# The low-rank layer of a four-part sequence kernel: its factors made by rank over 128 partitions, and the front's sums read out of PSUM

## The reference, cut to what matters

```python
# part 0, per batch row b (2 rows)
ae = layernorm(cond, ln_g, ln_b)                        # (2, 512)
h = gelu(ae @ w1 + b1)                                  # (2, 512)
xw = h @ w2 + b2                                        # (2, 8192), w2 is (512, 8192), 16.8 MB
x_a, x_b = split(xw, 2); each reshaped to (b, 512, 8)   # column index is d * 8 + rank
layer = base + einsum('bdr,bkr->bdk', x_a, x_b)         # (b, 512, 512)
x = x + (x + x @ layer)                                 # so 2 x + x @ layer
# part 1
x = x + tanh(x @ W_ih.T + (cond @ W_hh.T + b_hh + b_ih))
# parts 2 and 3, each: gates of x @ Wx + b + h @ Wh, 2048 steps, x = x + h of the step
```

## Time and profile before

| | us |
|---|---|
| median of 3 runs | 12192.23 |
| runs, lowest to highest | 12192.1 to 12194.81 |
| profiled execution, its own time | 12186.99 |
| profiled execution, span from first to last instruction | 12183.9 |

### The profile page before, as it was taken

One profiled execution on the slowest core, in us unless ns is written; L12 is line 12 of the kernel. 1 busy time (PEld: TensorE's weight loads), 2 busy tenths in 40 slices (PEclk: granted clock), 3 DMA queues, 4 the chain that ended last, 5 costly groups with the idle time before them and its releaser, 6 DMA issues.

```text
span 12183.9 us, 681007 instructions
## 1 busy us (share of the span) xinstructions
PE 11997.7 (98%) x429656; PEld 4439.7 (36%) x167512; DVE 7525.4 (62%) x34072; ACT 3039.0 (25%) x20584; POOL 1414.8 (12%) x5242
## 2 busy tenths in 40 slices
PE   7899999999999999999999999999999999999998
PEld 5433333333333343333343333343333343333333
DVE  4366666666666666666666666666666666666664
ACT  1122222222222222222222222222222222222221
POOL 4011111111111111111111111111111111111110
PEclk8999999999999999999999999999999999999999
DMA  4100000000000000000000000000000000000000
GB/s 147 37 6 6 6 6 6 6 6 6 6 6 6 6 6 6 6 6 6 6 6 6 6 6 6 6 6 6 6 6 6 6 6 6 6 6 6 6 6 4
DMA packets 382314, 123.89 MB, mean 10 GB/s; under 512 B 355654, under 2 KB 363910, under 8 KB 379308
## 3 DMA queue, kind: packets, MB, share of 16 engines
q1 hardware_dynamic: 364332, 46.45, 2.4%
q10 hardware_dynamic: 12544, 25.17, 0.6%
q0 software_dynamic: 2432, 8.39, 0.2%
HBM read 63.08 MB, written 16.84 MB: 7 GB/s over the span
## 4 chain that ended last, share of the span: by engine, by line
PE 96%; DVE 1%; ACT 0%; issue 0%; DVEq 0%; POOL 0%
PE gates L80 88%; PE proj L780 7%; DVE gates_t L912 0%; DVE pre L917 0%; ACT tanh_c L828 0%; ACT sig L823 0%; DVE prod L924 0%; DVE state L931 0%; DVE state L935 0%; DVE gc L927 0%; DVE state L938 0%; ACT gc L824 0%; DVEq L923 0%; DVEq L911 0%; DVE y_rows L888 0%
## 5 line engine op out<-in xcount | busy, mean ns | idle before, releaser
L80 PE MATMUL gates<-wh,state 128*12 128x256 bf16 x393216 | 11463.6, 273 | 93.4 <-DVE state L938 89.6
L80 PEld LDWEIGHTS gates<-wh,state 128*12 128x12 bf16 x131072 | 3302.1, 88 | 6625.9 <-issue 6410.2
L912 DVE STREAM_TRANSPOSE gates_t<-gates 128x256 f32<-128x256 f32 x4096 | 1843.8, 450 | 1586.1 <-PE gates L80 1581.5
L823 ACT ACTIVATE sig<-pre 128x16 f32<-128x16 f32 x4096 | 885.9, 216 | 7081.6 <-DVE pre L917 7081.6
L917 DVE TENSOR_REDUCE pre<-gates_t 128x24 f32<-128x96 f32 x4096 | 1340.4, 327 | 140.8
L924 DVE TENSOR_TENSOR prod<-sig,gc 128x16 f32<-128x16 f32 x4096 | 718.5, 175 | 1129.9 <-ACT gc L824 1028.4
L931 DVE TENSOR_TENSOR state<-sig,tanh_c 128x8 f32<-128x8 f32 x4096 | 690.5, 169 | 1123.9 <-ACT tanh_c L828 1123.9
L828 ACT ACTIVATE tanh_c<-gc 128x8 f32<-128x8 f32 x4096 | 854.3, 209 | 1711.6 <-DVE gc L927 1711.6
L840 POOL TENSOR_TENSOR x<-x1r,state 128x8 f32<-128x8 f32 x2048 | 433.3, 212 | 5436.6 <-DVE state L938 5436.6
L840 POOL TENSOR_TENSOR y<-x,state 128x8 f32<-128x8 f32 x2048 | 432.6, 211 | 5063.7 <-DVE state L938 5063.7
L819 ACT COPY gates_t<-area 128x32 f32<-128x32 f32 x4096 | 826.1, 202 | 20.5 <-POOL area L849 18.3
(11 more groups left out here) (81 smaller groups left out, 1243.5 us busy)
## 6 DMA issues: line engine op xcount, KB each, us to landing
w<-in_w ACTq DMA_DIRECT2D x8, 2048.0 KB, 16.6
out<-y_rows SPq DMA_DIRECT2D x1024, 8.0 KB, 1.9
wx<-in_x SPq DMA_DIRECT2D x16, 512.0 KB, 4.5
x_t_all<-x_t ACTq DMA_DIRECT2D x8, 1024.0 KB, 4.8
x1p<-x_t_all SPq DMA_DIRECT2D x128, 64.0 KB, 2.6
x1r<-x_t_all SPq DMA_DIRECT2D x128, 64.0 KB, 2.6
wx<-in_Wh POOLq DMA_DIRECT2D x8, 512.0 KB, 4.7
wx<-in_Wh POOLq DMA_DIRECT2D x16, 256.0 KB, 6.4
```

What stands on the lines that cost most here:

```text
L80: return pe.add_instruction(mybir.InstMatmult(name=nc.get_next_instruction_name(), engine=mybir.EngineType.PE, ins=[pe.lower_ap(moving), p ...
L823: act.activation(sig[l][:, 0:2 * HB], pre[l][:, 0:2 * HB], ACT.Sigmoid)
L912: dve.transpose(gates_t[l][:, :, NS * NB:], gates[l][:, 0:NMS * C].rearrange("p (m c) -> p m c", c=C)).then_inc(s["trans"], 1)
```

## The change

In `condition`:

- The product by `w2` puts the rank on the partitions. For rank r = 4 i + j, column tile j holds it at partition 32 j + 2 i + b for batch row b. The moving operand is `w2` read at a step of eight floats (`by_rank`); the two halves i are added into the same bank with two versions of the weights, `hid_p[:, 0]` and `hid_p[:, 1]`, whose columns are shifted by two. `b2` enters by a fifth matmul with a one-hot column (`select`). A product so has 2 x 5 x 4 = 40 matmuls of 128 columns.
- The pieces of x_b come first (`ORDER`), then those of x_a. A piece of x_b is copied out of PSUM into `xb`; a piece of x_a is copied twice, multiplied by a mask that keeps one batch row. After each piece of x_a its two layer matmuls follow over 128 partitions, and VectorE adds `base`. `xw_dram`, the stores, and the reload are gone.
- The hidden vector and the term of cond are computed with the vector as the weights and the matrix moving (`rows_by_tile`), turned once by a transpose.
- `w2` is asked for by SP, after `w1`, LayerNorm's vectors, `b1` and `b2`; x's first tile after the fourth piece, its second tile after the last. W_hh, W_ih, `b_ih`, `b_hh`, the gate biases and `base` are asked for by POOL, W_hh once `w1` and `b1` have landed.
- ScalarE loads its square root and gelu tables ahead by an activation on a spare value (`ahead`), and copies the turned W_hh and W_ih out of PSUM, which VectorE did. VectorE starts on cond's own semaphore.

In `front`: `x0_t` is made by one instruction, 2 x + PSUM; the tanh is written over its own PSUM bank, and `x1_t` is summed from there. The transposes of the next tile wait for `s_x1` in place of `s_tanh`.

The diff, cut to its core:

```diff
-    WC = W2N // NJ
-    ND = WC // RANK
+    NI = RANK // NJ
+    ND = W2N // RANK
+    HALF = NPIECE // 2
+    ORDER = [*range(HALF, NPIECE), *range(HALF)]
...
+        def by_rank(ap, i, j):
+            return ap.rearrange("p (d r) -> p r d", r=RANK)[:, NJ * i + j, :]
+        def of_piece(n):
+            return slice(ND * (n % HALF), ND * (n % HALF) + ND)
...
+                def second(k):
+                    dve.wait_ge(s_xw, k + 1)
+                    done(dve.tensor_copy(xb[:, of_piece(ORDER[k])], factor[k % 2][:, 0:ND]), f"xb{k}")
+                second(0)
+                second(1)
+                dve.wait_ge(s_term_r, 1)
+                done(dve.tensor_copy(rows[1][:, :], by_row[:, P:2 * P]), "term_r")
+                second(2)
+                dve.wait_ge(s_term_t, 1)
+                dve.wait_ge(s_bias, NBIAS * DMA)
                 for h in range(NH):
...
-                for n in range(NPIECE):
-                    dve.wait_ge(s_pe, J_XW + n)
-                    done(dve.tensor_tensor(xw[:, n, :, :], bank[4 + n % 2][:, 0:WC].rearrange("p (d r) -> p r d", r=RANK),
-                                           b2[:, n, :].rearrange("p (d r) -> p r d", r=RANK), ALU.add), f"xw{n}")
-                dve.wait_ge(s_base, DMA)
-                for k in range(NB * NH):
-                    b, h = divmod(k, NH)
-                    dve.wait_ge(s_pe, J_LAYER + k)
-                    done(dve.tensor_tensor(layer[b][:, h, :], bank[k % 4][:, :], base[:, h, :], ALU.add), f"layer{k}")
+                second(3)
+                dve.wait_ge(s_dve, V["mask"])
+                for k in range(HALF, NPIECE):
+                    n = ORDER[k]
+                    dve.wait_ge(s_xw, k + 1)
+                    for b in range(NB):
+                        step = dve.tensor_scalar(xa[:, b, of_piece(n)], factor[k % 2][:, 0:ND], mask[:, b:b + 1],
+                                                 None, ALU.mult)
+                        step.then_inc(s_factor, 1)
+                    if k == HALF:
+                        dve.wait_ge(s_base, DMA)
+                    for b in range(NB):
+                        dve.wait_ge(s_layer, NB * n + b + 1)
+                        dve.tensor_tensor(layer[b][:, n, :], bank[(NB * n + b) % 4][:, :], base[:, n, :],
+                                          ALU.add).then_inc(s_made, 1)
...
+                sp.wait_ge(s_zero, ZERO)
+                sp.dma_start(b2[0:NPIECE, :], ins["b2"].rearrange("(n i) -> n i", i=W2N)).then_inc(s_b2, DMA)
+                for k, n in enumerate(ORDER):
+                    if k >= NW2:
+                        sp.wait_ge(s_xw, k - NW2 + 1)
+                    load_blocked(sp, w2[k % NW2][:, :, :], ins["w2"][:, W2N * n:W2N * n + W2N], s_w2[k % NW2])
+                    if k == NW2 - 1:
+                        turn.load_rows(sp, 0)
                 sp.wait_ge(turn.s_turn, NH)
                 turn.load_rows(sp, 1)
...
+                pool.wait_ge(s_w1, 2 * DMA)
+                pool.dma_start(whh[:, :, :], ins["W_hh"].rearrange("(a p) i -> p a i", p=P)).then_inc(s_whh, DMA)
+                pool.dma_start(wih[:, :, :], ins["W_ih"].rearrange("(a p) i -> p a i", p=P)).then_inc(s_wih, DMA)
+                pool.wait_ge(s_zero, ZERO)
+                pool.wait_ge(s_ident, 2)
+                for i in range(NI):
+                    for b in range(NB):
+                        pool.tensor_copy(select[:, :, i, NB * i + b], ident[:, 0:NPIECE]).then_inc(s_select, 1)
+                load_bias(pool, bih_t[:, :], ins["b_ih"], s_bias)
+                load_bias(pool, bhh_t[:, :], ins["b_hh"], s_bias)
+                load_gate_bias(pool, keep["bias"][0][:, :], ins["b_l2"], s_bias)
+                load_gate_bias(pool, keep["bias"][1][:, :], ins["b_l3"], s_bias)
+                load_blocked(pool, base[:, :, :], ins["base"], s_base)
...
-                for n in range(NPIECE):
-                    if n == 1:
-                        act.wait_ge(s_w1, 2 * DMA)
-                    if n == NW2:
-                        act.wait_ge(s_dve, V["variance"])
-                        act.activation(stat[:, 3:4], stat[:, 2:3], ACT.Sqrt).then_inc(s_act, 1)
-                        act.wait_ge(s_pool, 4)
-                        act.wait_ge(s_w1, 2 * DMA)
-                        act.wait_ge(s_pe, J_HID)
-                        for h in range(NH):
-                            act.activation(hid_t[:, h, 0:NB], small[:, 32 + NB * h:32 + NB * h + NB], ACT.Gelu,
-                                           bias=b1_t[:, h:h + 1]).then_inc(s_act, 1)
-                    if n >= NW2:
-                        act.wait_ge(s_pe, J_XW + n - NW2)
-                    load_blocked(act, w2[n % NW2][:, :, :], ins["w2"][:, W2N * n:W2N * n + W2N], s_w2[n % NW2])
...
+                for k in range(4):
+                    act.wait_ge(s_turn, k + 1)
+                    act.copy(whh_t[:, k, :], bank[k][:, :]).then_inc(s_whh_t, 1)
+                for k in range(4):
+                    act.wait_ge(s_turn, 4 + k + 1)
+                    act.copy(wih_t[:, k, :], bank[k][:, :]).then_inc(s_wih_t, 1)
...
+                def rows_by_tile(out, columns, moving):
+                    for h in range(NH):
+                        for j in range(NJ):
+                            mm = pe.matmul(out[C * j:C * j + C, :], columns[:, h, :], block_cols(moving[:, h, :], j),
+                                           start=(h == 0), stop=(h == NH - 1),
+                                           tile_position=(0, C * j), skip_group_check=True)
+                    return mm
...
+                def product(k):
+                    n = ORDER[k]
+                    pe.wait_ge(s_w2[k % NW2], (k // NW2 + 1) * DMA)
+                    if 2 <= k < HALF + 2:
+                        pe.wait_ge(s_dve, V[f"xb{k - 2}"])
+                    elif k >= HALF + 2:
+                        pe.wait_ge(s_factor, NB * (ORDER[k - 2] + 1))
+                    to = factor[k % 2][:, 0:ND]
+                    for i in range(NI):
+                        for h in range(1 + NH):
+                            for j in range(NJ):
+                                columns = hid_p[:, i, h - 1, :] if h else select[:, n, i, :]
+                                moving = by_rank(w2[k % NW2][:, h - 1, :] if h else b2[:, :], i, j)
+                                mm = pe.matmul(to[C * j:C * j + C, :], columns, moving,
+                                               start=(i == 0 and h == 0), stop=(i == NI - 1 and h == NH),
+                                               tile_position=(0, C * j), skip_group_check=True)
+                    mm.then_inc(s_xw, 1)
...
+                pe.wait_ge(s_whh, DMA)
+                for k in range(4):
+                    turned(whh, k)
+                pe.wait_ge(s_b2, DMA)
+                pe.wait_ge(s_select, NI * NB)
+                pe.wait_ge(s_dve, V["hid_p"])
+                product(0)
+                pe.wait_ge(s_wih, DMA)
+                for k in range(4):
+                    pe.wait_ge(s_whh_t, k + 1)
+                    turned(wih, k)
+                product(1)
+                rows_by_tile(by_row[:, P:2 * P], cond_p, whh_t).then_inc(s_term_r, 1)
+                product(2)
+                pe.wait_ge(s_dve, V["term_r"])
+                pe.transpose(small[:, 2 * P:3 * P], rows[1][:, :], ident[:, :]).then_inc(s_term_t, 1)
+                pe.wait_ge(s_wih_t, 4)
+                turn.transpose(pe, 0, bank)
+                product(3)
+                pe.wait_ge(s_dve, V["xb3"])
                 pe.wait_ge(turn.s_copy, NH)
-                pe.wait_ge(s_back, 2 * DMA)
-                for k in range(NB * NH):
-                    b, h = divmod(k, NH)
-                    if k >= 4:
-                        pe.wait_ge(s_dve, V[f"layer{k - 4}"])
-                    pe.matmul(bank[k % 4][:, :], block_cols(xab[:, b, 0:D], h), xab[:, b, D:2 * D],
-                              start=True, stop=True).then_inc(s_pe, 1)
+                for k in range(HALF, NPIECE):
+                    n = ORDER[k]
+                    product(k)
+                    for b in range(NB):
+                        pe.wait_ge(s_factor, NB * n + b + 1)
+                        if NB * n + b >= 4:
+                            pe.wait_ge(s_made, NB * n + b - 3)
+                        pe.matmul(bank[(NB * n + b) % 4][:, :], xa[:, b, of_piece(n)], xb[:, :],
+                                  start=True, stop=True).then_inc(s_layer, 1)
...
-                                       (lambda h: pe.wait_ge(s_tanh, NH * (u - 1) + h + 1)) if u else None)
+                                       (lambda h: pe.wait_ge(s_x1, NH * (u - 1) + h + 1)) if u else None)
...
-                            step = act.activation(tanh_t[:, h, cols], banks(u, 2)[h][:, cols], ACT.Tanh,
+                            step = act.activation(banks(u, 2)[h][:, cols], banks(u, 2)[h][:, cols], ACT.Tanh,
...
```

(48 more changed lines are left out.)

133 lines of the change are left out of this document (52 added, 81 removed).

## The result

| | us |
|---|---|
| before, median of 5 runs | 12192.23 (12184.79 to 12194.81) |
| changed, median of 5 runs | 12135.34 (12133.75 to 12137.98) |
| ratio, 95% interval | 0.9954 (0.994 to 0.9969) |
| changed, profiled execution, own time and span | 12137.98, 12136.2 |

The change takes 56.9 us off the median. The forecast was 12129, the range 12115 to 12152.

A forecast was written before the change was run, and what follows sets the result against it. The recurrence, bound by TensorE, stays unedited; waits in condition and front were to shrink. Condition 30.5 us plus front 32 makes 62.5, taken as 63: 12192.2 - 63 = 12129 us, range 12115 to 12152.

The forecast's parts named there:

- Step 1: Front: sums reading one operand from PSUM take 0.69 us, so TensorE's stalls go; 32 us saved, bounds 28 to 34.
- warm start: Front's first matmuls run at full clock instead of slowly; front saving 34 us, half a microsecond added to the forecast sum.
- Step 2: Condition: with loads reordered and DMA queues kept full, the last piece of `w2` lands at 62.5 us instead of 72.9.
- Steps 3 and 4: Condition's tail after the last `w2` landing, including the price of strided reads: 7.5 us, between 5.6 and 13.
- the sign named for it: Start of the front's matmuls in the changed profile, expected at 64 to 76 us.
- Step 3: Condition after the last landing: product, masked copy, layer matmuls, base sum; 5.6 us at full clock, 9.7 at half.
- rival C: Condition: strided reads make TensorE the bound; slower than before from 12 us a product, 12231 at 17; chance 0.03 in full.
- formula 22 + 13 + 8P: End of condition if TensorE bounds it: start at 22 us, 13 for transposes and layers, eight products of P each.
- Step 5: Condition: biases and `base` asked for by POOL instead of SP stay hidden, costing nothing; bias landing between 20 and 45 us.
- Rivals A and D: Condition: POOL's bias and base loads late, 12135 to 12149; or `w2` pieces asked for late, 12144; together chance 0.16.
- B: Front: VectorE's stalls beside POOL stay, leaving 31 us of saving, 12162 us; chance 0.05.

The follow-up runs named there:

- e7: Changed kernel with the front's sum as two instructions again, each with one operand in PSUM; 12141.19 us, a single run.
- e2: New `condition` of the change with the `front` of the kernel before; 12169.98 us, ratio 0.9983.
- e8: Changed kernel with the tanh written to SBUF again, so only `x1_t`'s sum has two SBUF operands; 12136.13 us, a single run.
- e3: Changed kernel with products reading 128 adjacent columns of `w2` and `b2` instead of every eighth (wrong columns, same work); 12126.49 us, ratio 0.9947.
- e5: The changed kernel once more, unedited, on another round of runs; 12138.18 us, ratio 0.9955.
- e6: Changed kernel with TensorE's list reordered: product 0 before W_hh's transposes, products ahead of the previous piece's layer matmuls; 12132.49 us, ratio 0.9951.

## Why the prediction came out as it did

*Step 1, the front: right, a little over its upper end.* 32 us were forecast with 34 for a warm start; 34.8 came. The reason given, the pair of SBUF operands beside POOL, is shown by e7 (two instructions without the pair: no stall), e2 (the pair: 12.20 us for one) and the sums at 692 ns once POOL has stopped. Both new forms were priced at 0.69 and take 0.69. What the step had too coarse: it took the slow first tile as likely to stay, and it named the tanh as part of the remedy, which e8 shows to be worth nothing.

*Step 2, the last landing: right.* 62.5 was forecast, and the last piece landed at 62.0. The average rate from 4 to 63 us was 384 GB/s where 385 was taken. W_hh's transposes began at 18.27 (18 forecast), product 0 ended at 26.7 (27).

*Steps 3 and 4, the tail: the term that was mis-sized.* 7.5 us were forecast from the last landing to the front, between 5.6 and 13; 19.2 came, outside the step's own bounds, so condition ended at 81.2 in place of 70, and the sign named for it, front matmuls from 64 to 76 us, was missed. The forecast put a product between 2.4 and 8.0 us and took it a third of the way, at about 4.3, where 4.9 was measured; the price itself was nearly met. What failed is what was made of it: the forecast let TensorE wait for the last landing, and TensorE came to the last piece 10.8 us after it. Step 3 weighed products and layers against the 5.2 us between landings only to settle the clock, and only at 2.4 us a product. At 4.9, with 1.98 for the layers and the hand-over to the masked copy, a piece takes 7.24 us of TensorE. Four of them from 51.02 end at 80, however early `w2` is there. This is rival C's mechanism, TensorE as the bound, at a price at which the change still gains; the forecast gave C a chance only at prices that end within the noise of no change or slower. Its formula 22 + 13 + 8P with P = 4.9 gives 74.2, and what it left out are TensorE's waits: 2.57 us for x, 0.34 for `w2`, about 0.5 at each of four masked copies, 0.4 for `xb`, 1.05 to the block's end, 6.3 in all, which makes 80.5. e3 shows the size of the step without the stride: products take 2.4 us, the front begins 7.1 us after the last landing, at 69.33, and 64.0 us are gained where 63 were forecast. But even there TensorE did not wait for the last piece; its list and the landing were within about a microsecond of each other, so that the 7.5 us fit owes something to luck. VectorE's factor of 1.76 came near TensorE's 2; no run shows that the two have one cause, and the 1.76 also holds what a VectorE instruction costs at any length (a copy of 8 columns takes 0.17 us). The choice of a third was not argued from a row, and the end to which the skill's rule pointed should have been carried through the period of a piece.

*Step 5, the moved queues: right.* The six gate biases took POOL 4.75 us to ask for, not 23.32, hterm followed at 39.75 with no wait, and `base` was there for the first sum at 57.66. Rivals A and D did not happen, nor did B. A's own sum was off: 55 to 65 us and four times 4.2 and 1 make 73 to 83, not 76 to 88.

*Together*: condition gave 11.2 us less than forecast and the front 2.3 more (34.8 against 32.5 with the warm start), 8.9 us short by the profiled stages and 6.3 by the medians, inside the range, whose upper part was there for A and for the stride. That the total stands inside although condition ended 5 us outside its bounds is in part luck: the range reached to 12152 for rival A, which was not the case. The prediction also named a recurrence longer by over 5 us as a contradiction, and by the two profiles it is 6.4 longer; the same kernel again (e5) has 11810.7 and e6, with the same recurrence, 11804.3, so a difference of this size comes without an edit.

## What to carry to other kernels

When a wait for a transfer is shortened, work out the period of the loop behind it on each engine with the operands as they will be read: here a step of 32 bytes doubled TensorE's fp32 products and made TensorE the bound of the stage's second half, and the stage gave 19 us in place of the 30 forecast. Beside a busy POOL, look at where VectorE's operands lie before counting its instructions, and mend first the sum that another engine waits for. Work that stands in line behind a late transfer is worth moving ahead of it once its engine is the bound.

## What the runs showed of the hardware

A TensorE product on fp32 read at steps of 1, 2, 4 and 8 floats took 1.06, 1.12, 2.04 and 2.08 us for 32 instructions of 128 columns, four side by side. In e2 VectorE's sum of two SBUF operands stood from 114.70 to 126.90 us, while POOL ran seven instructions of 1.0 to 3.6 us, one behind the other, from 115.11 to 126.35; it was not done until their row was. The sum with one operand in PSUM took 0.69 us beside the same POOL work (e7), and the sum of two SBUF operands 0.69 us with POOL idle (before, 248 to 370 us). POOL asked for six element-wise loads in 4.75 us; in the kernel before, the same six held SP's queue for 23.32.
